# A recommender's first dense layer: block sums moved from VectorE to GpSimd, gates in halves, chunks centred earlier

## The reference

```python
scores = jnp.einsum('bhd,bd->bh', hist_emb, user_emb)
user_his_emb = jnp.einsum('bh,bhd->bd', scores, hist_emb)
x = jnp.concatenate([items_emb, user_his_emb, user_emb], axis=1)   # 384 wide
x = _dice(_batchnorm(x @ W1 + b1, g1, be1), a1)                    # 1024 wide
x = _dice(_batchnorm(x @ W2 + b2, g2, be2), a2)                    # 512 wide
return x @ W3 + b3
```

## Time and profile before

| what | value |
|---|---|
| timed runs | 1004.77 us median of 3 (1000.77 to 1005.12) |
| profiled execution | 1015.52 us, its span 1013.7 us |
| mean granted clock of TensorE over the span | 0.758 |
| busy share of the span | PE 64%, DVE 52%, ACT 36%, POOL 49% |
| matmul groups of the dense stage | L1544 (`product`) x576, 113.3 us; L1559 (`average`) x64, 11.0 us |

### The profile page before, as it was taken

The page is one execution under the profiler, slowest core; times in us unless marked ns, Lnnn a source line. Parts: engine busy times, 40 slices in busy tenths (PEclk is TensorE's granted clock), DMA queues, the critical chain, the costliest instruction groups (busy, mean ns, idle before and its releaser), DMA issues.

```text
span 1013.7 us, 17230 instructions
## 1 busy us (share of the span) xinstructions
PE 653.8 (64%) x3753; PEld 606.6 (60%) x3753; DVE 522.8 (52%) x1353; ACT 360.5 (36%) x884; POOL 495.0 (49%) x561
## 2 busy tenths in 40 slices
PE   4563665637473846566566475756665569999998
PEld 3552555537373736465566364745664469888887
DVE  7653444344353625353445254544434536999758
ACT  3122232322231414132223142332233247787556
POOL 6655544545455453636354635545544524290036
PEclk8676776767587666767677667768777779999999
DMA  7111111111111111111111111111111110000000
GB/s 215 40 38 39 37 34 35 37 37 37 37 35 39 30 44 25 44 27 44 30 40 32 44 26 39 36 32 39 38 34 35 42 22 1 2 1 0 1 1 2
DMA packets 17241, 34.65 MB, mean 34 GB/s; under 512 B 8104, under 2 KB 8400, under 8 KB 17168
## 3 DMA queue, kind: packets, MB, share of 16 engines
q0 software_dynamic: 14208, 29.13, 11.7%
q1 hardware_dynamic: 2960, 4.67, 1.4%
HBM read 33.76 MB, written 0.01 MB: 33 GB/s over the span
## 4 chain that ended last, share of the span: by engine, by line
PE 45%; another core or an unknown queue 19%; issue 18%; ACTq 8%; ACT 6%; DVE 3%; DVEq 0%; PEldq 0%; POOL 0%; POOLq 0%
PE ps L1486 14%; PE ps L1544 10%; PE ps L1407 6%; PE ps L1423 5%; ACTq L1236 3%; ACT scaled L1236 3%; PE ps L1473 3%; ACTq L1257 2%; PE ps L1495 1%; ACTq L389 1%; ACTq L390 1%; PE ps L1559 1%; PE ps L1428 1%; PE ps L1386 1%
## 5 line engine op out<-in xcount | busy, mean ns | idle before, releaser
L520 POOL DMA_INDIRECT rows<-in_L_rec_user_table_dram,slot_idx x432 | 412.1, 954 | 388.3 <-ACT scaled L1236 260.6
L1486 PE MATMUL ps<-ident,scaled 128*128 128x128 f32 x984 | 211.7, 381 | 225.8 <-ACT scaled L1236 171.9
L1486 PEld LDWEIGHTS ps<-ident,scaled 128*128 128x128 f32 x984 | 186.8, 278 | 249.4 <-issue 221.8
L1236 ACT ACTIVATE scaled<-rows,work 128x128 f32 (+1 forms) x492 | 176.5, 401 | 271.5 <-remote 191.1
L812 DVE TENSOR_TENSOR prod<-rows,ps 128x512 f32<-128x512 f32 x122 | 83.7, 686 | 168.4 <-POOLq L527 88.1
L689 DVE SCALAR_TENSOR_TENSOR h<-ps,col_no 128x1024 f32<-128x1024 f32 (+1 forms) x34 | 39.2, 1161 | 159.0 <-ACT ranked L1205 88.1
L1544 PE MATMUL ps<-h,w 128*128 128x256 f32 (+1 forms) x576 | 113.3, 356 | 1.0 <-DVE h L1042 1.0
L1407 PE MATMUL ps<-wide,h 128*128 128x104 f32 x512 | 98.6, 369 | 14.6 <-issue 14.6
L1544 PEld LDWEIGHTS ps<-h,w 128*128 128x128 f32 x576 | 99.6, 190 | 12.8 <-issue 1.2
L1407 PEld LDWEIGHTS ps<-wide,h 128*128 128x128 f32 x512 | 94.3, 281 | 21.2 <-issue 21.2
L818 DVE TENSOR_REDUCE work<-prod 128x512 f32 (+1 forms) x122 | 83.7, 686 | 38.8 <-issue 25.5
(11 more groups left out here) (217 smaller groups left out, 784.7 us busy)
## 6 DMA issues: line engine op xcount, KB each, us to landing
rows<-in_L_rec_user_table_dram,slot_idx POOLq DMA_INDIRECT x432
w<-in_L_rec_W_dram SPq DMA_DIRECT2D x1, 2048.0 KB, 17.5
w<-in_L_rec_W_dram SPq DMA_DIRECT2D x1, 1536.0 KB
h<-in_r_history_users_dram SPq DMA_DIRECT2D x2, 400.0 KB, 3.4
wide<-in_L_rec_user_table_dram,own_idx POOLq DMA_INDIRECT x5
wide<-in_L_rec_item_table_dram,own_idx POOLq DMA_INDIRECT x5
last_row<-in_L_rec_user_table_dram SPq DMA_DIRECT2D x1, 64.0 KB
last_item<-in_L_rec_item_table_dram SPq DMA_DIRECT2D x1, 64.0 KB
```

The source lines that it names most:

```text
L520: nc.gpsimd.indirect_dma_start(rows[:, s, :], None, user_table, bass.IndirectOffsetOnAxis(slot_idx[:, s:s + 1], 0)).then_inc(landed[s], 16)
L1236: nc.scalar.activation(scaled[:, j, :], rows[:, bass.ds((g & (GROUPS - 1)) * GROUP + j, 1), :], ACT.Copy, scale=score[:, bass.ds(g * GROUP ...
L1486: nc.tensor.matmul(pooled_ps, scaled[:, j, :], ident[:, :], start=False, stop=False, skip_group_check=True).then_inc(slot_summed, 1)
```

## The change

- `DIRECT` goes from 4 to 3, so chunk 3's mean too comes from `average_sum`. `halve_blocks` moves as a whole from VectorE to GpSimd, behind normalise(c) for c from 3 on. GpSimd's waits for `dice_done` ahead of normalise(c) go, and `back` and `at_place` are made after its loop.
- `scale` and `open_gate` work in two halves for every chunk, where they did so for chunk 0 only.
- VectorE's order: mix(0) ahead of halve_squares(1), mix(1) between the parts of halve_squares(2), center(3) ahead of invert(2) where it stood behind scale(2), count_chunk(c - 2) ahead of invert(c).
- ScalarE's order: square(1) ahead of take_root(0), normalise(3) in two parts around it and open_gate(0); square(c) writes chunk 1's squares beside chunk 0's; a dummy sigmoid (`load_gates`) behind take_root(1) and take_root(2); square(3) ahead of open_gate(2); in the loop normalise(c + 2) ahead of keep_layer2(c - 2) and take_root(c).
- TensorE's order: average(3) goes; product(0, 0) comes ahead of variance(1) and product(1, 0) ahead of variance(2); average_sum(3) stands between product(1, 2) and product(1, 3).
- In the tail turn(0) and turn(1) stand ahead of the count of tile 8, where they stood ahead of that of tile 12.

```diff
--- before.py
+++ after.py
@@ -50,7 +50,7 @@
     N_SPANS = len(spans)
     NARROW = 2
-    DIRECT = 4
+    DIRECT = 3
     QUARTER = 4 * P
...
@@ -408,6 +409,11 @@
         def dev_of(c):
             return dev[c % 3][:, 0:M1 * spans[c][1]]
+        def squares_of(c):
+
+            at = M1 * spans[0][1] if c == 1 else 0
+            return dev_sq[:, at:at + M1 * spans[c][1]]
+
         def by_block(flat, m):
             return flat.rearrange("p (m b) -> p m b", m=m)
@@ -556,17 +562,31 @@
                     nc.gpsimd.tensor_scalar(h1[:, k, chunk(c)], h1[:, k, chunk(c)], scale1[:, k:k + 1],
                                             shift1[:, k:k + 1], ALU.mult, ALU.add).then_inc(normed_other, 1)
+            def halve_blocks(c):
+
+                w = spans[c][1]
+                half = by_block(col_tree[:, 0:4 * w], 4)
+                pool.wait_ge(normed_act, sum(M1 - len(by_other(x)) for x in range(c + 1)))
+                pool.wait_ge(normed_other, others(c))
+                if c > DIRECT:
+                    pool.wait_ge(col_summed, c - DIRECT)
+                nc.gpsimd.tensor_tensor(half, h1[:, 0:4, chunk(c)], h1[:, 4:8, chunk(c)], ALU.add).then_inc(col_step, 1)
+                pool.wait_ge(col_step, 2 * (c - DIRECT) + 1)
+                nc.gpsimd.tensor_tensor(half[:, 0:2, :], half[:, 0:2, :], half[:, 2:4, :], ALU.add).then_inc(col_step, 1)
+                pool.wait_ge(col_step, 2 * (c - DIRECT) + 2)
+                if c > DIRECT:
+                    pool.wait_ge(avg_ready, c)
+                nc.gpsimd.tensor_tensor(col_sum[:, 0:w], half[:, 0, :], half[:, 1, :], ALU.add).then_inc(col_summed, 1)
+
             for c in range(1, N_SPANS):
-                if c > 3:
-
-                    pool.wait_ge(dice_done, 2 * (c - 3))
                 normalise(c)
-                if c == N_SPANS - 2:
-                    pool.wait_ge(whose_kept, TILES)
-                    for t in range(TILES):
-                        nc.gpsimd.tensor_scalar(back[:, t, :], col_no[:, :], whose[:, t, 0:1], None, ALU.is_equal).then_inc(backs_made, 1)
-                        nc.gpsimd.tensor_scalar(at_place[:, t, :], col_no[:, 0:TILES], whose[:, t, 1:2], None,
-                                                ALU.is_equal).then_inc(backs_made, 1)
+                if c >= DIRECT:
+                    halve_blocks(c)
+            pool.wait_ge(whose_kept, TILES)
+            for t in range(TILES):
+                nc.gpsimd.tensor_scalar(back[:, t, :], col_no[:, :], whose[:, t, 0:1], None, ALU.is_equal).then_inc(backs_made, 1)
+                nc.gpsimd.tensor_scalar(at_place[:, t, :], col_no[:, 0:TILES], whose[:, t, 1:2], None,
+                                        ALU.is_equal).then_inc(backs_made, 1)
             pool.wait_ge(bn_ready[1], 1)
             k, of = M2 - 1, slice(QUARTER, 2 * QUARTER)
@@ -990,7 +1010,7 @@
             def halve_squares(c, first):
                 w = spans[c][1]
-                sq = by_block(dev_sq[:, 0:M1 * w], M1)
+                sq = by_block(squares_of(c), M1)
                 if first:
                     dve.wait_ge(squared, c)
                     nc.vector.tensor_tensor(sq[:, 0:4, :], sq[:, 0:4, :], sq[:, 4:8, :], ALU.add).then_inc(sq_step, 1)
@@ -1001,23 +1021,6 @@
                     dve.wait_ge(var_ready, c)
                     nc.vector.tensor_tensor(sq_sum[:, 0:w], sq[:, 0, :], sq[:, 1, :], ALU.add).then_inc(sq_summed, 1)
-            def halve_blocks(c, first):
-                w = spans[c][1]
-                half = by_block(col_tree[:, 0:4 * w], 4)
-                if first:
-                    dve.wait_ge(normed_act, sum(M1 - len(by_other(x)) for x in range(c + 1)))
-                    dve.wait_ge(normed_other, others(c))
-                    if c > DIRECT:
-                        dve.wait_ge(col_summed, c - DIRECT)
-                    nc.vector.tensor_tensor(half, h1[:, 0:4, chunk(c)], h1[:, 4:8, chunk(c)], ALU.add).then_inc(col_step, 1)
-                else:
-                    dve.wait_ge(col_step, 2 * (c - DIRECT) + 1)
-                    nc.vector.tensor_tensor(half[:, 0:2, :], half[:, 0:2, :], half[:, 2:4, :], ALU.add).then_inc(col_step, 1)
-                    dve.wait_ge(col_step, 2 * (c - DIRECT) + 2)
-                    if c > DIRECT:
-                        dve.wait_ge(avg_ready, c)
-                    nc.vector.tensor_tensor(col_sum[:, 0:w], half[:, 0, :], half[:, 1, :], ALU.add).then_inc(col_summed, 1)
-
             def invert(c):
                 w = spans[c][1]
                 dve.wait_ge(rooted, c + 1)
...
@@ -1038,7 +1041,7 @@
                 if c == 0:
                     dve.wait_ge(par_ready, 6)
                 for half in (slice(0, 4), slice(4, M1)):
-                    dve.wait_ge(gated, c + 2 if c else half.stop // 4)
+                    dve.wait_ge(gated, 2 * c + half.stop // 4)
                     nc.vector.scalar_tensor_tensor(h1[:, half, chunk(c)], by_block(dev_of(c), M1)[:, half, :], over[:, 0:1],
                                                    h1[:, half, chunk(c)], ALU.add, ALU.mult).then_inc(dice_done, 1)
@@ -1052,28 +1055,24 @@
             center(1)
             invert(0)
             scale(0)
+            mix(0)
             halve_squares(1, True)
             halve_squares(1, False)
-            mix(0)
             center(2)
             invert(1)
             scale(1)
             halve_squares(2, True)
+            mix(1)
             halve_squares(2, False)
-            mix(1)
+            center(3)
             invert(2)
             scale(2)
-            center(3)
             mix(2)
             for c in range(3, N_SPANS):
                 halve_squares(c, True)
-                if c + 1 < N_SPANS:
-                    halve_blocks(c + 1, True)
                 halve_squares(c, False)
-                if c + 1 < N_SPANS:
-                    halve_blocks(c + 1, False)
+                count_chunk(c - 2)
                 invert(c)
-                count_chunk(c - 2)
                 scale(c)
                 if c + 1 < N_SPANS:
                     center(c + 1)
@@ -1265,7 +1264,7 @@
                 nc.scalar.activation(pooled_T[:, :], pooled_ps, ACT.Copy).then_inc(pooled_kept, 1)
             act.wait_ge(dried, 1)
-            nc.scalar.activation(root_dry[:, :], ones[:, 0:1], ACT.Sqrt)
+            nc.scalar.activation(root_dry[:, :], ones[:, 0:1], ACT.Sqrt).then_inc(root_used, 1)
             keep_layer1(TILES - 1, 0)
             keep_layer1(TILES - 1, 4)
@@ -1274,8 +1273,8 @@
             nc.scalar.activation(bn_s[:, :], bn_v[:, :], ACT.Sqrt, bias=bn_eps[:, 0:1], scale=2.0 / TILES).then_inc(bn_rooted[0], 1)
             act.wait_ge(bn_ready[0], 1)
-            def normalise(c):
-                for k in range(M1):
+            def normalise(c, of=range(M1)):
+                for k in of:
                     if k not in by_other(c):
                         nc.scalar.activation(h1[:, k, chunk(c)], h1[:, k, chunk(c)], ACT.Identity,
                                              bias=shift1[:, k:k + 1], scale=scale1[:, k:k + 1]).then_inc(normed_act, 1)
@@ -1290,22 +1289,20 @@
             def square(c):
                 if c > 1:
                     act.wait_ge(sq_summed, c - 1)
-                elif c:
-                    act.wait_ge(var_ready, 1)
-                else:
+                elif c == 0:
                     act.wait_ge(stream_over, 1)
                 act.wait_ge(dev_ready, c + 1)
                 n = M1 * spans[c][1]
                 if c:
-                    nc.scalar.activation(dev_sq[:, 0:n], dev_of(c), ACT.Square).then_inc(squared, 1)
+                    nc.scalar.activation(squares_of(c), dev_of(c), ACT.Square).then_inc(squared, 1)
                 else:
                     for half in (slice(0, n // 2), slice(n // 2, n)):
                         nc.scalar.activation(dev_sq[:, half], dev_of(c)[:, half], ACT.Square).then_inc(first_squared, 1)
             def open_gate(c):
-                n = M1 * spans[c][1] // (1 if c else 2)
-                for k in range(1 if c else 2):
-                    act.wait_ge(arg_ready, c + 2 if c else k + 1)
+                n = M1 * spans[c][1] // 2
+                for k in range(2):
+                    act.wait_ge(arg_ready, 2 * c + k + 1)
                     of = dev_of(c)[:, k * n:(k + 1) * n]
                     nc.scalar.activation(of, of, ACT.Sigmoid).then_inc(gated, 1)
@@ -1320,22 +1317,32 @@
             normalise(0)
             normalise(1)
             square(0)
-            normalise(3)
+            normalise(3, range(0, 1))
+            square(1)
             take_root(0)
-            square(1)
             open_gate(0)
+            normalise(3, range(1, M1))
+            def load_gates(n):
+
+                act.wait_ge(root_used, n)
+                nc.scalar.activation(root_dry[:, :], ones[:, 0:1], ACT.Sigmoid).then_inc(root_used, 1)
+
             take_root(1)
+            load_gates(1)
             square(2)
             open_gate(1)
```

(39 more changed lines are left out.)

## The result

The changed kernel took 1011.72 us (median of 6 runs, 1009.91 to 1013.88), the kernel before 1004.94 us (median of 6, 1000.77 to 1005.60). The ratio is 1.0062, with a 95% interval of 1.0040 to 1.0084: slower by 0.6%. The profiled execution took 1009.91 us, its span 1008.1 us.

A forecast was written before the change was run, and what follows sets the result against it. It took TensorE's own work to bound the dense layers, so what counted was product(2, 0)'s start and the clock. Product order +2.4, clock +2.5, ring 0, tail 0: +4.9 on 1004.77 gives 1009.7 us, range 1004 to 1014.

The forecast's parts named there:

- center(3) behind the late sum: On VectorE, center(3) waits 4.7 us for average_sum(3), holding up invert(2); TensorE pauses 6.0 us before product(2, 0).
- The product order term: Chunk 2's products on TensorE end at 892.1 instead of 889.7 us: +2.4 us, average(3)'s saving included.
- The clock term: TensorE's clock falls in the 6.0 us pause and stays at half speed for 5.1 us afterwards: +2.5 us.
- Afterwards: Step on later chunks: ScalarE and VectorE keep up with TensorE, 0 more; GpSimd stretches VectorE 0.2 us a chunk at most.
- The sum: Product order +2.4, clock +2.5, ring 0 and tail 0 make +4.9 us for the kernel.
- GpSimd's price: halve_blocks' 1792 elements on GpSimd cost between 3.2 and 14.9 us, taken as 5 to 7, hidden for chunk 3.
- The ring: ScalarE's and VectorE's round per chunk takes 15.1 us against TensorE's 14.7; its lead covers three rounds: 0, narrowly.
- The tail: Moving the two turns from behind the twelfth count to behind the eighth: 0, between -0.4 and +0.2 us.
- Rival B: center(3) delays nothing, pause before product(2, 0) under 2 us, average_sum(3) done by about 865.4: -3 us, 1001.8; chance 0.10.
- Rival C: GpSimd's additions come late, or VectorE stretched by GpSimd makes the ring the bound: +7 to +8, 1012.5 us; chance 0.15.

The follow-up runs named there:

- e1: Changed kernel with average_sum(3) ahead of product(1, 0); stage (first normalise(0) to last product's end) 131.7 us, ratio 0.9986 to the kernel before.
- e2: Changed kernel with center(3) back behind scale(2) and open_gate(2) ahead of square(3); stage 132.8 us, ratio 1.0003 to the kernel before.
- e7: Kernel before with center(3) ahead of invert(2) and nothing else; stage 133.7 us, ratio 1.0019 to the kernel before.
- e3: Changed kernel with 25 unit-matrix products keeping TensorE busy in the pause before product(2, 0); stage 137.8 us, ratio 1.0040 to the kernel before.
- e5: Changed kernel with normalise(c + 2) back behind keep_layer2 and take_root in ScalarE's loop; stage 137.2 us, ratio 1.0053 to the kernel before.
- e4: Changed kernel with the two turns back behind the count of tile 11; stage 138.8 us, tail 37.2 us, ratio 1.0070 to the kernel before.
- e11: e1 with GpSimd's last addition of chunk c, from 4 on, only behind sq_sum(c - 1); stage 130.8 us, ratio 0.9975 to the kernel before.
- e9: e3 with GpSimd beginning halve_blocks(c), c from 5 on, only when sq_sum(c - 2) is made; stage 135.8 us, ratio 1.0025 to the kernel before.
- e10: e1 together with e5's edit, normalise(c + 2) back behind take_root; stage 131.7 us, ratio 0.9995 to the kernel before.

## Why the prediction came out as it did

Forecast 1009.7 us, +4.9, range 1004 to 1014; measured 1011.72, inside it, and slower. The ratio, 0.6%, lies just beyond the 0.5% at which the prediction divides "slower" from "same", with 0.47 for each; the interval, 0.40 to 0.84%, reaches over that bound.

- **center(3) behind the late sum: right.** A wait of 4.86 us was measured for 4.7, a pause of 6.02 for 6.0, a chain of 7.96 from average_sum(3) to product(2, 0) for 7.8. e1, e2 and e7 show that it needs both the place of center(3) and that of average_sum(3).
- **The product order term, +2.4: too small.** Without the clock's loss and GpSimd's, the stage is 135.8, +3.0. average_sum(3) was through 0.5 us later than worked out (@26.06, where the next product starts, for @25.6). 0.3 of it is that product(1, 0), behind its short wait, took 2.1 us from its start to the next row's, for 1.8 without a wait; the working had left that out.
- **The clock term, +2.5: the fall was right, its effect was not.** It fell in the pause, was back 4.0 us after work resumed, for 5.1, and took 2.0 us from product(2, 0), for 2.5. But in the changed kernel taking the fall away gives nothing (e3). The step that failed stands under "Afterwards": "GpSimd's additions could stretch VectorE's operations; the rows put this at 0.2 us a chunk at most". One addition of VectorE's was stretched by 2.0 us, and it stood just where the slow product hid it. The reading of the rows was low as well: beside GpSimd's operations of before, VectorE's addition for sq_sum took 0.50 and 0.67 us for 0.42, and with the one into col_sum (0.58) that makes 0.2 to 0.4 us a chunk. But those operations of GpSimd read one tensor each; no addition of two ran there, so no row could have given the 2.0 us.
- **The sum, +4.9, against +5.0 in the stage** is thus nearer than its terms, which is luck: +3.0 and then the later of two delays of 2.0, where +2.4 and +2.5 were added.
- **GpSimd's price: right.** 2.50 + 1.27 + 0.74 = 4.5 us, within the bounds of 3.2 and 14.9, though below the 5 to 7 that were taken; for chunk 3 it was through 8.5 us before average_sum(3) ran. The estimate of 3.9 us from the Trainium skill (GPSIMD Engine Reference, section 3.1) was near too; the trace is 15% above it.
- **The ring: right.** mix(c) came every 14.93 us (15.1 worked out) against TensorE's 14.7, and its lead held; no wait in chunks 3 to 8, and e5 shows no gain of its own from undoing it. In e2, with TensorE earlier, it seems to have caught up, for 0.4 us. **The tail: right**, 37.15 against 37.17 us, and e4.
- **The rest of the median.** The medians differ by 6.8 us, the interval is 4.0 to 8.4 us, the stage and the tail explain 5.0. The start of the dense stage lay between 830.7 and 843.8 us in the profiles of these chips, so the gather stage scatters by more than what is left. Whether part of it is the change's was not tried.

Rival B's condition, average_sum(3) done early, is e1: it did decide the sign of the stage (131.7 against 132.8). Rival C was right in kind, GpSimd stretches VectorE, though at another place and beside the clock's loss, not on top of it.

## What to carry to other kernels

In a stream that runs strictly in order, look for the pair: an operation moved ahead on one engine whose producer was moved back on another; here the stage grew by 5 us although 14 matmuls were saved, and moving the producer by three products gives it back. When a delay is removed and the time stays, look for a second one that ends at the same place, and take away both before giving up the first. Work handed to GpSimd was free here only while VectorE didn't read two tensors from SBUF on the critical path; a wait that starts it behind that work cost nothing and saved 0.9 us (e11 against e1).

## What was unexpected in the hardware

An addition of two tensors on GpSimd that had begun 0.25 us earlier stopped VectorE's for its whole length: 0.42 us became 2.46, ending 0.3 us after GpSimd's 2.42 us were over. e3 and e4 show the same (2.45 us each), and e9 took it away by order alone. The Trainium skill (GPSIMD Engine Reference, section 8) says that the two contend where VectorE has two SBUF inputs, and the trace agrees: center and scale, which read one operand from PSUM, kept their 2.28 and 2.35 us beside GpSimd's additions. In the other direction GpSimd's two blocks of 256 columns took 3.54 for 1.10 us in e10.

The clock's return is not one figure. After a pause of 6.02 us, product(2, 0) took 5.16, 5.68, 5.78 and 6.74 us in four profiles, so the same fall cost 1.5 to 3.1 us. By the windows the granted clock was back at 1.00 about 3.0, 4.0, 4.2 and 6.2 us after work resumed. In the dense stage TensorE does the same work ahead of the pause in all four (the third comes to it 0.6 us later). What sets the return is not shown.

On one of the chips used, the kernel before took 752.20 us instead of 1005. The dense stage is no shorter there: e11's was as long as worked out, and its last row of 112 matmuls takes 24.34 us as on the others. But the dense stage starts at 580 us instead of 833, so the gather stage is shorter. The view of ScalarE's line that scales rows, for the changed kernel and then for e11:

```profile
L1235 ACTq ALU_OP  x525: 4/35/711, 70.3 to 826.1; - x175
```

```profile
L1236 ACTq ALU_OP  x525: 35/35/43, 52.3 to 572.7; - x175
```

ACTq is ScalarE's sequencer, ALU_OP an operation on its registers; the three numbers behind the colon are the shortest, median and longest of one in ns. It takes up to 711 ns in the first profile (1397 in that of the kernel before, on one of the slower chips too) and never over 43 on this one; the median is 35 in both. What makes it long was not tried, nor how much of the 253 us lies in it.
